# Laying out key and value blocks by DMA, and another order of an attention round

## The chip, the core and the metric

The kernel runs on one core of a Trainium2 chip. The metric is the device time of one execution in microseconds (us). The core has TensorE (PE, matmuls and transposes), VectorE (DVE), ScalarE (ACT), GpSimd (POOL) and SyncE (SP), which here only issues DMA transfers. Each engine runs its own program in order; semaphores tie them together.

## The reference

Two layers over x of 16 batches x 256 tokens x 256 features (4096 tokens), with a context of 16 x 77 x 256:

```
q = layernorm(x) @ Wq + bq;  k, v = split(ctx @ Wkv + bkv)       # 16 heads of 16
out = softmax(q @ k^T / 4) @ v                                    # per batch and head, 77 keys
x = x + out @ Wp + bp
xf = layernorm(layernorm(x)) (with gain and bias)
scores, idx = top_k(xf @ router_w, 2);  gate = softmax(scores)
x = x + sum over the 2 experts of gate * expert(xf)               # 8 experts, hidden 1024
expert(y) = clip((h1 * silu(clip(h2)))) @ Wo + bo,  h1 = ln(y) @ W1 + b1,  h2 = ln(y) @ W2 + b2
```

All in float32. The kernel splits operands of the large matmuls into a high part (float32r) and a low part (the rest) and adds three products.

## The kernel before

The work is cut into 32 tiles of 128 tokens, two for each batch. The first part of the program is a pipeline of **rounds**, numbered -5 to 40. In round i TensorE computes the scores of tile i, the transposed probabilities and the values of tile i-1, the projection of tile i-2, the transposes of `xn` for tile i+3 and of `xf` for tile i-4, and the router's logits of tile i-5. Once for each batch there are also, in an even round, the transposed context, keys and values of batch nb = i//2 + 1, and, in the odd round after it, the queries of that batch. From round 32 on the rounds are interleaved with the first expert tile; then come expert tiles alone. Weights of the first experts are loaded from round 28 on.

Each engine's order in a round is written out by hand: `round_first`, `round_second` and `round_third` for TensorE, a `round_ops` each for ScalarE and VectorE, and loops over the rounds for SP and POOL. The two banks of PSUM called misc are handed round in a fixed order (`misc_turns`): a user of a bank waits until the user before it has been read.

**Scores.** A batch's keys stand in `k_blocks`: on each partition, for each of four heads of a group, the 77 keys if the partition belongs to that head and zeros if not, so that one matmul gives four heads' scores (128 x 308). Scores of half a tile (`m` = 0 or 1) are two such groups in two of three banks, so the second half waits until VectorE has read one bank of the first half (`less_max`). Before, ScalarE writes the high parts of `k_blocks` by copies scaled with a 0/1 mask (line 802), and POOL the low parts by a multiplication with the mask (line 622). The first scores of a batch (line 1537, s = m = 0) wait for both.

**Values.** The 16 x 77 = 1232 keys of a batch stand in 10 blocks of 128 rows; in `v_blocks` each block has 3 places for the heads that it may touch, zero where a row is another head's. A row is 17 floats (16 values and a 1 for the softmax sum). Before, VectorE adds the bias into `v_sb` (77 partitions; line 1189), SP stores it to `v_flat` in HBM (line 456), loads it back in blocks (lines 444 and 447, `v_rep`), and POOL multiplies with masks (line 667). `v_blocks`, `v_sb` and `k_blocks` have two buffers each. `values` (line 1615) of a tile runs in the round after its scores; it ends `round_second`.

**SP's order in a round** before: in an odd round the x load for tile i+7, `load_values`, the store of `x1`; in an even round the x load, the store of `x1`, `store_values` and the context load for batch nb+2.

Of the kernel before, what the change touches and what calls it, by code (L numbers as in the profile page):

```python
# [120 lines left out]
C_KMASK = C_IOTA + P  # L121
C_VMASK = C_KMASK + HPB
C_TOKEN = C_VMASK + KB * BLOCK_HEADS
# [20 lines left out]

def constants():
# [6 lines left out]
    c[:, C_KMASK:C_KMASK + HPB] = (p[:, None] // HD) % HPB == np.arange(HPB)[None, :]  # L152
    for i in range(KB):
        first, n = block_heads(i)
        for j in range(BLOCK_HEADS):
            c[:, C_VMASK + i * BLOCK_HEADS + j] = (i * P + p) // CTX == first + j
# [31 lines left out]
def misc_turns():  # L188

    order = []  # L190
    for i in range(FIRST_ROUND, LAST_ROUND + 1):
        even, nb = i % 2 == 0, i // 2 + 1
        batch = 0 <= nb < BATCH
        uses = [("ctx", nb)] if batch and even else []
        uses += [("attn", i - 2)] if 0 <= i - 2 < NT else []
        uses += [("q", nb)] if batch and not even else []
        uses += [("proj", i - 2)] if 0 <= i - 2 < NT else []
        uses += [("place", i // 2 - 4)] if even and 0 <= i // 2 - 4 < PAIRS else []
        uses += [("xn", i + 3)] if 0 <= i + 3 < NT else []
        uses += [("logits", i - 5)] if 0 <= i - 5 < NT else []  # L200
        uses += [("k", nb), ("v", nb)] if batch and even else []
        uses += [("xf", i - 4)] if 0 <= i - 4 < NT else []
        uses += [("rows", 0), ("rows", 1)] if i == NT - 2 else []
        order += [(i, u) for u in uses]
    turns, last, side = {}, [None, None], 0
    for i, u in order:
        side = 1 if i >= OVERLAP + LAG else 1 - side
        turns[u] = (side, last[side])
        last[side] = u
    return turns, last  # L210


def build(nc, a, out):
    with ExitStack() as ctx:
# [8 lines left out]
        def sems(name, n):  # L223
# [3 lines left out]
        v_flat = nc.dram_tensor("v_flat", [BATCH, KEYS, VW], F32, kind="Internal").ap()  # L227
# [4 lines left out]
        f_vstore, f_vload = sems("f_vstore", 2), sems("f_vload", 2)  # L232
# [4 lines left out]
        (bq_ready, setup_ready, half_ready, zeros_ready, ones_ready, mv_ready) = (  # L237
            sem(n) for n in ("bq_ready", "setup_ready", "half_ready", "zeros_ready",
                             "ones_ready", "mv_ready"))
# [5 lines left out]
        (k_low, k_low_spread, q_low, v_added, v_spread, max_found, less_max, recip_made, attn_made,  # L245
         best_made, best_index) = (
            sem(n) for n in ("k_low", "k_low_spread", "q_low", "v_added", "v_spread", "max_found",
                             "less_max", "recip_made", "attn_made", "best_made", "best_index"))
        (ctx_t_out, k_out, k_high, k_high_spread, xn_t_out, q_out, q_high, exp_made, probs_t_out,
         attn_t_out, xf_t_out, logits_out) = (  # L250
            sem(n) for n in ("ctx_t_out", "k_out", "k_high", "k_high_spread", "xn_t_out", "q_out",
                             "q_high", "exp_made", "probs_t_out", "attn_t_out", "xf_t_out",
                             "logits_out"))
# [70 lines left out]
        k_h = sb("k_h", [P, DC, CTX], F32R)  # L324
        k_l = sb("k_l", [P, DC, CTX])
# [4 lines left out]
        v_rep = [sb(f"v_rep{i}", [P, KB, VW]) for i in range(2)]  # L330
# [92 lines left out]
        def sync_program(e):  # L423
# [15 lines left out]
            def load_values(b):  # L439
                e.wait_ge(f_vstore[b % 2], 16 * (b // 2 + 1))  # L440
                if b >= 2:
                    e.wait_ge(v_spread, 6 * (b - 1))
                full = (KB - 1) * P
                e.dma_start(v_rep[b % 2][:, 0:KB - 1, :],
                            v_flat[b][0:full, :].rearrange("(i p) d -> p i d", p=P)).then_inc(
                                f_vload[b % 2], 16)
                e.dma_start(v_rep[b % 2][0:TAIL, KB - 1, :], v_flat[b][full:KEYS, :]).then_inc(
                    f_vload[b % 2], 16)
# [4 lines left out]

            def store_values(b):
                e.wait_ge(v_added, b + 1)
                e.dma_start(v_flat[b].rearrange("(h k) d -> k h d", h=HEADS),
                            v_sb[b % 2][:, :, :]).then_inc(f_vstore[b % 2], 16)
# [71 lines left out]
            for i in range(FIRST_ROUND, OVERLAP + 2):  # L529
# [67 lines left out]
        def pool_program(e):  # L597
# [19 lines left out]
            def spread_low_keys(b):  # L617
                e.wait_ge(k_low, b + 1)
                if b >= 2:
                    e.wait_ge(scores_mm, SCORES_OF_BATCH * (b - 1))  # L620
                for m in range(DC):
                    e.tensor_tensor(
                        k_blocks[b % 2][:, 1, m, :, :],
                        k_l[:, m, :].unsqueeze(1).broadcast_to([P, HPB, CTX]),
                        const[:, C_KMASK:C_KMASK + HPB].unsqueeze(2).broadcast_to([P, HPB, CTX]),
                        ALU.mult).then_inc(k_low_spread, 1)

# [31 lines left out]
            def spread_values(b):  # L659
                e.wait_ge(f_vload[b % 2], 32 * (b // 2 + 1))  # L660
                if b >= 2:
                    e.wait_ge(values_mm, 2 * b - 2)
                vm = const[:, C_VMASK:C_VMASK + KB * BLOCK_HEADS].rearrange(
                    "p (i j) -> p i j", i=KB)
                for j in range(BLOCK_HEADS):
                    for parts, lo, hi in ((P, 0, KB - 1), (TAIL, KB - 1, KB)):
                        e.tensor_tensor(
                            v_blocks[b % 2][0:parts, lo:hi, j, :], v_rep[b % 2][0:parts, lo:hi, :],
                            vm[0:parts, lo:hi, j:j + 1].broadcast_to([parts, hi - lo, VW]),
                            ALU.mult).then_inc(v_spread, 1)  # L670

# [13 lines left out]

            e.memset(half[:, :], -0.5).then_inc(half_ready, 1)
# [49 lines left out]
            for i in range(FIRST_ROUND, LAST_ROUND + 1):  # L736
                nb = i // 2 + 1
                batch = 0 <= nb < BATCH
                if batch and i % 2:
                    spread_low_keys(nb)  # L740
# [4 lines left out]
                if batch and i % 2:  # L745
                    spread_values(nb)
# [27 lines left out]
        def act_program(e):  # L774
# [8 lines left out]
            def keys(b):  # L783
                ps = misc_of("k", b)
                e.wait_ge(k_mm, b + 1)
                if b:
                    e.wait_ge(k_low, b)
                    e.wait_ge(k_high_spread, HPB * b)
# [6 lines left out]
                e.activation(k_h[:, :, :], k_t[:, :, :], ACTF.Copy).then_inc(k_high, 1)  # L795

            def spread_high_keys(b):
                e.wait_ge(k_high, b + 1)
                if b >= 2:
                    e.wait_ge(scores_mm, SCORES_OF_BATCH * (b - 1))  # L800
                for h in range(HPB):
                    e.activation(k_blocks[b % 2][:, 0, :, h, :], k_h[:, :, :].bitcast(F32),
                                 ACTF.Copy, scale=const[:, C_KMASK + h:C_KMASK + h + 1]).then_inc(
                                     k_high_spread, 1)
# [179 lines left out]
            def round_ops(i):  # L984
# [5 lines left out]
                if batch and even:  # L990
                    ctx_t(nb)
                if 0 <= i - 3 < NT:
                    make_y(i - 3)
                if 0 <= i - 2 < NT:
                    attn_t_copy(i - 2)
                if before:
                    probs_t_copy(i - 1, 1)
                if batch and not even:
                    spread_high_keys(nb)
                    queries(nb)  # L1000
                if before:
                    probs_t_copy(i - 1, 2)
                if 0 <= i + 3 < NT:
                    xn_t_copy(i + 3)
                if 0 <= i - 5 < NT:
                    make_z(i - 5)
                if 0 <= i < NT:
                    exp_scores(i, 1)
                    exp_scores(i, 0)
                if 0 <= i - 5 < NT:  # L1010
                    logits_copy(i - 5)
                if batch and even:
                    keys(nb)
                if 0 <= i - 4 < NT:
                    xf_t_copy(i - 4)
                if 0 <= i + 4 < NT:
                    make_xn(i + 4)
# [58 lines left out]
        def dve_program(e):  # L1076
# [27 lines left out]
            def low_keys(b):  # L1104
                e.wait_ge(k_high, b + 1)
                if b:
                    e.wait_ge(k_low_spread, 2 * b)
                e.tensor_tensor(k_l[:, :, :], k_t[:, :, :], k_h[:, :, :].bitcast(F32),
# [73 lines left out]
            def add_value_bias(b):  # L1182
# [4 lines left out]
                if b >= 2:  # L1187
                    e.wait_ge(f_vstore[b % 2], 16 * (b // 2))
# [170 lines left out]
            def round_ops(i):  # L1359
# [16 lines left out]
                if i == EARLY_TILES + 7:  # L1376
                    early_slots()
                if 0 <= i < NT:
# [23 lines left out]
                if batch and even:  # L1402
                    add_value_bias(nb)
# [113 lines left out]
        def pe_program(e):  # L1517
# [86 lines left out]
            def values(i):  # L1604
# [3 lines left out]
                if i % 2 == 0:  # L1608
                    e.wait_ge(v_spread, 6 * (b + 1))
# [269 lines left out]
```

## Time and profile before

| | |
|---|---|
| median of 3 runs | 1061.42 us (1059.45 to 1069.49) |
| the profiled execution | 1053.62 us, its span 1051.8 us |
| granted clock, mean | 0.947 of full speed |
| TensorE / VectorE / ScalarE / POOL busy | 91% / 75% / 68% / 42% of the span |
| transfers issued by SP for the values of one batch | 3 |

The span is the time from the first to the last instruction. A granted clock of 1.0 is 2.4 GHz for TensorE and 0.5 is 1.2 GHz. In a timeline row the first number is the start (us from the span's start), the second the length of a merged run of instructions, then engine, line, operation, what is written and read, and the count; the bracket is the idle time of that engine just before, and what ended it.

### The profile page before, as it was taken

To read this page: it belongs to the slowest core of one execution; us is meant where nothing else is said; L and a number is where in the kernel's file an instruction comes from. 1 tells how busy PE (TensorE), PEld (TensorE's weight loads), DVE (VectorE), ACT (ScalarE), POOL (GpSimd) and SP (SyncE) were. 2 spreads that over 40 slices of the span, in tenths; PEclk is the share of its full clock that TensorE was granted. 3 is DMA by queue.
4 is the path that set the end of the run, shared out by engine and by line. 5 is a ranking of instruction groups with operands and counts; after the bars stand their busy time and mean duration, and the time that the engine had idled before them with its cause. 6 is when DMAs were issued, how large, how long until landed. Compare 5 with 4: busy or idle time off the path is not lost.

```text
span 1051.8 us, 19535 instructions
## 1 busy us (share of the span) xinstructions
PE 962.4 (91%) x6372; PEld 848.9 (81%) x6372; DVE 790.0 (75%) x1775; ACT 710.2 (68%) x1418; POOL 442.7 (42%) x683
## 2 busy tenths in 40 slices
PE   5999989999987879899999999999999999999893
PEld 4887777777776768688989898888888888889892
DVE  3676777687674677777888787878787878788883
ACT  3777767676665555666777777767676767676781
POOL 4554766777665374512332323223231414050422
PEclk8998989899887789999999999999999999999996
DMA  5312222322226047534656564555555555555644
GB/s 136 50 37 44 61 51 62 76 64 56 52 51 179 21 166 243 147 106 145 168 134 178 127 183 128 165 144 156 153 147 163 139 162 127 175 116 187 169 148 142
DMA packets 124827, 130.42 MB, mean 124 GB/s; under 512 B 50016, under 2 KB 109104, under 8 KB 124592
## 3 DMA queue, kind: packets, MB, share of 16 engines
q1 hardware_dynamic: 111280, 111.13, 35.3%
q0 software_dynamic: 13440, 17.97, 9.6%
q8 instruction: 54, 0.88, 0.3%
q14 instruction: 53, 0.43, 0.1%
HBM read 105.32 MB, written 25.88 MB: 125 GB/s over the span
## 4 chain that ended last, share of the span: by engine, by line
PE 59%; DVE 19%; issue 8%; ACT 5%; DMA 4%; POOL 2%; SPq 1%; another core or an unknown queue 1%; DVEq 0%; ACTq 0%; POOLq 0%
PE bank L1745 25%; PE bank L1775 12%; PE bank L1615 5%; PE bank L1537 3%; DVE wl L1414 3%; DVE maxes L1094 2%; PE bank L1555 2%; PE bank L1582 2%; PE bank L1641 2%; PE bank L1636 2%; DMA raw<-in_W 1%; ACT wh L922 1%; DVE yo L1463 1%; PE bank L1724 1%; DVE xl L1420 1%
## 5 line engine op out<-in xcount | busy, mean ns | idle before, releaser
L730 POOL DMA_INDIRECT out_rows<-yo,token x72 | 125.9, 1748 | 430.3 <-ACT yo L981 415.6
L1745 PE MATMUL bank<-xh,wh 128*128 128x512 f32 (+1 forms) x768 | 267.1, 348 | 17.5 <-DVE hid L1445 14.9
L1745 PE MATMUL bank<-xh,wl 128*128 128x512 f32 (+1 forms) x768 | 262.2, 341 | 0.8 <-issue 0.8
L1745 PE MATMUL bank<-xl,wh 128*128 128x512 f32 (+1 forms) x768 | 261.9, 341 | 0.0
L1414 DVE TENSOR_TENSOR wl<-raw,wh 128x1024 fp32r<-128x1024 f32 x148 | 178.3, 1221 | 37.4 <-ACT wh L922 37.2
L1745 PEld LDWEIGHTS bank<-xh,wh 128*128 128x128 f32 x768 | 147.2, 192 | 37.1 <-DVE hid L1445 19.4
L1775 PE MATMUL bank<-wh,hh 128*128 128x256 f32 x576 | 163.7, 284 | 4.8 <-DVE yo L1463 3.7
L1775 PE MATMUL bank<-wl,hh 128*128 128x256 f32 x576 | 162.5, 282 | 1.5 <-issue 1.5
L1775 PE MATMUL bank<-wh,hl 128*128 128x256 f32 x576 | 162.5, 282 | 0.0
L1745 PEld LDWEIGHTS bank<-xh,wl 128*128 128x128 f32 x768 | 146.7, 191 | 19.0 <-issue 1.2
L922 ACT ACTIVATE wh<-raw 128x1024 fp32r<-128x1024 f32 x148 | 152.8, 1053 | 6.5 <-DMA raw<-in_W 6.5
L1745 PEld LDWEIGHTS bank<-xl,wh 128*128 128x128 f32 x768 | 146.7, 191 | 12.4
L1454 DVE TENSOR_TENSOR hl<-hid,hh 128x512 fp32r<-128x512 f32 x144 | 98.9, 687 | 46.3 <-ACT hh L975 27.0
L1775 PEld LDWEIGHTS bank<-wh,hh 128*128 128x128 f32 x576 | 109.9, 191 | 10.7 <-DVE yo L1463 6.1
L1775 PEld LDWEIGHTS bank<-wl,hh 128*128 128x128 f32 x576 | 110.0, 191 | 4.8 <-issue 1.1
L1775 PEld LDWEIGHTS bank<-wh,hl 128*128 128x128 f32 x576 | 109.9, 191 | 1.2 <-issue 1.2
L975 ACT ACTIVATE hh<-hid 128x512 fp32r<-128x512 f32 x144 | 90.1, 626 | 28.3 <-DVE hid L1449 25.1
L957 ACT ACTIVATE gate_in<-bank,par 128x512 f32<-128x512 f32 x96 | 65.2, 680 | 48.6 <-PE bank L1745 41.8
L981 ACT ACTIVATE yo<-yo,gate 128x256 f32<-128x256 f32 x72 | 31.4, 500 | 92.2 <-DVE yo L1469 92.2
L968 ACT ACTIVATE gate_in<-gate_in 128x512 f32<-128x512 f32 x144 | 89.5, 622 | 0.0
L679 POOL DMA_INDIRECT z_rows<-z,slot x64 | 65.5, 1024 | 42.5 <-issue 26.2
L1615 PEld LDWEIGHTS bank<-v_blocks,probs_t 128*128 128x128 f32 (+1 forms) x640 | 78.8, 202 | 0.2
(161 smaller groups left out, 1922.5 us busy)
## 6 DMA issues: line engine op xcount, KB each, us to landing
raw<-in_W SPq DMA_DIRECT2D x52, 1024.0 KB, 5.0
raw<-in_Wo SPq DMA_DIRECT2D x25, 1024.0 KB
zg<-z_rows SPq DMA_DIRECT2D x12, 520.0 KB, 6.5
xs<-in_x SPq DMA_DIRECT2D x32, 128.0 KB, 3.2
out_rows<-x SPq DMA_DIRECT2D x32, 128.0 KB, 1.7
zg<-z_rows SPq DMA_DIRECT2D x14, 260.0 KB, 3.7
bo_row<-in_bo SPq DMA_DIRECT2D x26, 128.0 KB, 3.5
z_rows<-in_pad SPq DMA_DIRECT2D x8, 260.0 KB
```

The source lines that it names most:

```text
L679: e.indirect_dma_start(out=z_rows, out_offset=bass.IndirectOffsetOnAxis(ap=slot[:, 2 * p + t, k:k + 1], axis=0), in_=z[p % ZR][:, t, :], i ...
L730: e.indirect_dma_start(out=out, out_offset=bass.IndirectOffsetOnAxis(ap=token[j % 4][:, s:s + 1], axis=0), in_=yo[:, s, :], in_offset=None ...
L922: e.activation(wh[j % 2][:, w, c, :], raw[w][:, c, :], ACTF.Copy).then_inc(w_high, 1)
L957: e.activation(dst[:, :], ps[:, 0:WIDTH], ACTF.Identity, bias=par[j % PR][:, X_B2 + u:X_B2 + u + 1]).then_inc(gate_out, 1)
L968: e.activation(gate_in[n % 3][:, :], gate_in[n % 3][:, :], ACTF.Silu).then_inc(silu_made, 1)
L975: e.activation(hh[n % HR][:, :], hid[n % 2][:, :], ACTF.Copy).then_inc(hid_high, 1)
L1414: e.tensor_tensor(wl[j % 2][:, w, c, :], raw[w][:, c, :], wh[j % 2][:, w, c, :].bitcast(F32), ALU.subtract).then_inc(w_low, 1)
L1454: e.tensor_tensor(hl[n % HR][:, :], hid[n % 2][:, :], hh[n % HR][:, :].bitcast(F32), ALU.subtract).then_inc(hid_low, 1)
L1537: mm = e.matmul(score_bank[(u0 + g) % 3][:, 0:HPB * CTX], qs[b % 2][g * HALF:(g + 1) * HALF, m, s * P:(s + 1) * P], k_blocks[b % 2][g * HA ...
L1615: mm = e.matmul(value_bank[:, first * VW:(first + nh) * VW], probs_t[i % 2][0:size, k, :], v_blocks[b % 2][0:size, k, 0:nh, :].rearrange(" ...
L1745: mm = e.matmul(ps[:, h * cols:(h + 1) * cols], ws[j % 2][:, w, c, m * P:(m + 1) * P], xx[j % 2][:, c, 0:cols], start=(h == 0 and c == 0 a ...
L1775: mm = e.matmul(down_bank[s // 2][:, (s % 2) * D:(s % 2 + 1) * D], hs[r][:, at:at + P], ws[q][:, 2, m // 4, (m % 4) * D:(m % 4 + 1) * D], ...
```

## The change

The blocks are zeroed once by POOL, before anything else in its program. From then on transfers write only the parts that aren't zero, from SBUF to SBUF: 8 for the keys of a batch (a head's 16 partitions, high and low part together) and 25 for the values (`VALUE_PARTS`: one for each head, and one more where a head's 77 rows cross a block's border). All 33 are issued by SP in the odd round, values first. `values` of a batch waits for its 25 and the first scores for its 8. The masks, `v_flat`, `v_rep`, and the work of lines 622, 667 and 802 are gone.

In TensorE's round, keys and values move from `round_third` to the end of `round_first`, that is, before the second half of the scores; the context is transposed a round earlier, in `round_third` of the odd round; the logits move before the projection; the transposes of `xn` move behind `values`. ScalarE's and VectorE's orders follow: `exp_scores` of the first half now comes before the queries, and the bias add before VectorE's second softmax half.

```diff
+def value_parts(h):
+    parts, k = [], 0
+    while k < CTX:
+        i, at = divmod(h * CTX + k, P)
+        n = min(CTX - k, P - at)
+        parts.append((k, n, i, at, h - block_heads(i)[0]))
+        k += n
+    return parts
+VALUE_PARTS = [(h,) + part for h in range(HEADS) for part in value_parts(h)]
...
@@ sync_program
-            def load_values(b):
-                e.wait_ge(f_vstore[b % 2], 16 * (b // 2 + 1))
+            def spread_keys(b):
+                e.wait_ge(k_low, b + 1)
+                if b == 0:
+                    e.wait_ge(blocks_ready, 4)
                 if b >= 2:
-                    e.wait_ge(v_spread, 6 * (b - 1))
...
+                    e.wait_ge(scores_mm, SCORES_OF_BATCH * (b - 1))
+                for h in range(HPC):
+                    part = slice(h * HD, (h + 1) * HD)
+                    e.dma_start(k_blocks[b % 2][part, :, :, h % HPB, :].bitcast(F32),
+                                k_parts[part, :, :, :].bitcast(F32)).then_inc(f_kblocks[b % 2], 16)
+            def spread_values(b):
+                e.wait_ge(v_added, b + 1)
+                if b == 0:
+                    e.wait_ge(blocks_ready, 4)
+                if b >= 2:
+                    e.wait_ge(values_mm, 2 * b - 2)
+                for h, k, n, i, at, j in VALUE_PARTS:
+                    e.dma_start(v_blocks[b % 2][at:at + n, i, j, :],
+                                v_sb[b % 2][k:k + n, h, :]).then_inc(f_vblocks[b % 2], 16)
...
                 if batch and i % 2:
-                    load_values(nb)
+                    spread_values(nb)
+                    spread_keys(nb)
+                    if nb + 2 < BATCH:
+                        load_ctx(nb + 2)
                 if 0 <= i - 2 < NT:
                     store_x1(i - 2)
-                if batch and i % 2 == 0:
-                    store_values(nb)
-                    if nb + 2 < BATCH:
-                        load_ctx(nb + 2)
@@ pool_program
+            for i in range(2):
+                e.memset(k_blocks[i][:, :, :, :, :].bitcast(F32), 0.0).then_inc(blocks_ready, 1)
+                e.memset(v_blocks[i][:, :, :, :], 0.0).then_inc(blocks_ready, 1)
...
-                if batch and i % 2:
-                    spread_low_keys(nb)
...
-                if batch and i % 2:
-                    spread_values(nb)
@@ pe_program, scores
-                    e.wait_ge(k_high_spread, HPB * (b + 1))
-                    e.wait_ge(k_low_spread, 2 * (b + 1))
+                    e.wait_ge(f_kblocks[b % 2], 16 * HPC * (b // 2 + 1))
@@ pe_program, the rounds
-                if batch and even:
-                    transpose_ctx(nb)
                 if 0 <= i - 2 < NT:
                     transpose_attn(i - 2)
                 if 0 <= i - 1 < NT:
                     transpose_probs(i - 1, 1)
+                if batch and even:
+                    keys_values(nb)
                 if batch and not even:
                     queries(nb)
...
             def round_second(i):
                 if 0 <= i < NT:
                     scores(i, 1)
                 if 0 <= i - 1 < NT:
                     transpose_probs(i - 1, 2)
+                if 0 <= i - 5 < NT:
+                    route_logits(i - 5)
                 if 0 <= i - 2 < NT:
                     project(i - 2)
...
-                if 0 <= i + 3 < NT:
-                    transpose_xn(i + 3)
                 if 0 <= i - 1 < NT:
                     values(i - 1)
...
             def round_third(i):
-                if 0 <= i - 5 < NT:
-                    route_logits(i - 5)
-                if 0 <= nb < BATCH and even:
-                    keys_values(nb)
+                if i % 2 and 0 <= i // 2 + 2 < BATCH:
+                    transpose_ctx(i // 2 + 2)
+                if 0 <= i + 3 < NT:
+                    transpose_xn(i + 3)
                 if 0 <= i - 4 < NT:
                     transpose_xf(i - 4)
```

## Rows read from the trace of the kernel before

**Rows 1.** The page, busy time of each engine.

```profile
PE 962.4 (91%) x6372; PEld 848.9 (81%) x6372; DVE 790.0 (75%) x1775; ACT 710.2 (68%) x1418; POOL 442.7 (42%) x683
```

**Rows 2.** Windows: length, then busy us of each engine, clock, DMA share, GB/s.

```profile
100.00:200.00 100.00, 90.44 (x668) 76.30 (x664) 74.61 (x265) 71.59 (x195) 69.41 (x126) 0.94 0.29 62
...
200.00:203.00 3.00, 3.00 (x13) 2.66 (x14) 0.84 (x5) 0.75 (x4) 1.99 (x3) 0.50 0.12 44
```

**Rows 3.** Timeline of TensorE, the first scores of batch 0 and of batch 15.

```profile
20.04 0.63 PE L1537 MATMUL bank<-k_blocks,q_h 64*128 64x308 f32 x2 [3.50 <-POOL k_blocks L622]
...
320.05 0.41 PE L1537 MATMUL bank<-k_blocks,q_h 64*128 64x308 f32 x2
```

**Rows 4.** Timeline of TensorE, one period from an even round's scores, clock 1.0.

```profile
213.90 0.41 PE L1537 MATMUL bank<-k_blocks,q_h 64*128 64x308 f32 x2
...
216.81 0.41 PE L1537 MATMUL bank<-k_blocks,q_h 64*128 64x308 f32 x2 [0.84 <-DVE probs L1100]
...
219.63 0.44 PE L1600 MATMUL bank<-const,xn 128*128 128x128 f32 x2 [0.83 <-DVE x L1131]
219.90 2.32 PE L1615 MATMUL bank<-v_blocks,probs_t 128*128 128x34 f32 x20
222.06 0.59 PE L1625 MATMUL bank<-router,xf_t 128*128 128x8 f32 x4
222.50 1.09 PE L1636 MATMUL bank<-c_t,wk 128*128 128x77 f32 x8
...
224.30 0.38 PE L1649 MATMUL bank<-const,xf 128*128 128x128 f32 x2
...
233.32 0.41 PE L1537 MATMUL bank<-k_blocks,q_h 64*128 64x308 f32 x2
```

**Rows 5.** Timeline of TensorE, keys and values to the xf transposes, clock 0.5.

```profile
200.39 1.97 PE L1636 MATMUL bank<-c_t,wk 128*128 128x77 f32 x8
...
203.86 0.63 PE L1649 MATMUL bank<-const,xf 128*128 128x128 f32 x2
```

**Rows 6.** Groups by line, 100 to 300 us; then POOL's timeline in round 29.

```profile
L667 POOL TENSOR_TENSOR v_blocks<-v_rep,const 128x153 f32<-128x153 f32 (+1 forms) x60 | 18.6, 342 | 3.7 <-DMA v_rep<-v_flat 3.4 <-DVE mv L1147 0.2
L802 ACT ACTIVATE k_blocks<-k_h,const 128x154 fp32r<-128x154 f32 x40 | 13.6, 420 | 0.0
...
323.40 2.80 POOL L667 TENSOR_TENSOR v_blocks<-v_rep,const 128x153 f32<-128x153 f32 x6 [5.37 <-DMA v_rep<-v_flat]
```

**Rows 7.** Timeline of SP's issues, in rounds and at the program's start.

```profile
204.55 0.32 SPq L456 DMA_DIRECT2D v_flat<-v_sb  x1
204.92 0.81 SPq L433 DMA_DIRECT2D cs<-in_ctx  x1
...
209.41 0.39 SPq L444 DMA_DIRECT2D v_rep<-v_flat  x1
...
5.46 0.47 SPq L470 DMA_DIRECT2D rows<-in_bv  x1
5.97 0.43 SPq L470 DMA_DIRECT2D rows<-in_bp  x1
```

**Rows 8.** DMA issues (KB, us to landing); then line 522, ns min/median/max.

```profile
out_rows<-x SPq DMA_DIRECT2D x32, 128.0 KB, 1.7
...
v_rep<-v_flat SPq DMA_DIRECT2D x16, 76.5 KB, 2.4
...
v_rep<-v_flat SPq DMA_DIRECT2D x16, 5.3 KB, 2.3
...
L522 SPq DMA_DIRECT2D zg<-z_rows x26: 37/384/390, 319.6 to 1011.5; - x26
```

**Rows 9.** Timelines of VectorE and POOL at the program's start.

```profile
15.62 0.42 DVE L1189 TENSOR_TENSOR v_sb<-bank,rows 77x256 f32<-77x256 f32 x1 [7.72 <-DMA rows<-in_ln_b]
...
0.77 0.31 POOL L687 MEMSET zeros<- 128x256 f32 x1
...
5.33 0.19 POOL L636 TENSOR_TENSOR root<-mv,const 128x3 f32<-128x3 f32 x1 [4.12 <-DVE mv L1157]
```

More of the change, by code:

```diff
@@ L120 @@
 C_IOTA = C_TRI + P
-C_KMASK = C_IOTA + P
-C_VMASK = C_KMASK + HPB
-C_TOKEN = C_VMASK + KB * BLOCK_HEADS
+C_TOKEN = C_IOTA + P
 C_THR_E = C_TOKEN + NT
@@ L151, in constants @@
     c[:, C_IOTA:C_IOTA + P] = p[None, :]
[L152 to L156, printed above, removed]
     c[:, C_TOKEN:C_TOKEN + NT] = p[:, None] + P * np.arange(NT)[None, :]
@@ L193, in misc_turns @@
         batch = 0 <= nb < BATCH
-        uses = [("ctx", nb)] if batch and even else []
-        uses += [("attn", i - 2)] if 0 <= i - 2 < NT else []
+        uses = [("attn", i - 2)] if 0 <= i - 2 < NT else []
+        uses += [("k", nb), ("v", nb)] if batch and even else []
         uses += [("q", nb)] if batch and not even else []
+        uses += [("logits", i - 5)] if 0 <= i - 5 < NT else []
         uses += [("proj", i - 2)] if 0 <= i - 2 < NT else []
         uses += [("place", i // 2 - 4)] if even and 0 <= i // 2 - 4 < PAIRS else []
+        uses += [("ctx", nb + 1)] if 0 <= nb + 1 < BATCH and not even else []
         uses += [("xn", i + 3)] if 0 <= i + 3 < NT else []
-        uses += [("logits", i - 5)] if 0 <= i - 5 < NT else []
-        uses += [("k", nb), ("v", nb)] if batch and even else []
         uses += [("xf", i - 4)] if 0 <= i - 4 < NT else []
@@ L244, in build @@
                              "xf_summed", "xf_var", "z_made", "rstd_step", "rstd_made"))
[L245 to L253, printed above, removed]
+        (k_low, q_low, v_added, max_found, less_max, recip_made, attn_made, best_made,
+         best_index) = (
+            sem(n) for n in ("k_low", "q_low", "v_added", "max_found", "less_max", "recip_made",
+                             "attn_made", "best_made", "best_index"))
+        (ctx_t_out, k_out, k_high, xn_t_out, q_out, q_high, exp_made, probs_t_out, attn_t_out,
+         xf_t_out, logits_out) = (
+            sem(n) for n in ("ctx_t_out", "k_out", "k_high", "xn_t_out", "q_out", "q_high",
+                             "exp_made", "probs_t_out", "attn_t_out", "xf_t_out", "logits_out"))
         (ctx_t_mm, k_mm, v_mm, xn_t_mm, q_mm, scores_mm, probs_t_mm, values_mm, attn_t_mm, proj_mm,
@@ L323, in build @@
         k_t = sb("k_t", [P, DC, CTX])
-        k_h = sb("k_h", [P, DC, CTX], F32R)
-        k_l = sb("k_l", [P, DC, CTX])
+        k_parts = sb("k_parts", [P, 2, DC, CTX], F32R)
         xn = [sb(f"xn{i}", [P, D]) for i in range(2)]
@@ L329, in build @@
         v_sb = [sb(f"v_sb{i}", [CTX, HEADS, VW]) for i in range(2)]
-        v_rep = [sb(f"v_rep{i}", [P, KB, VW]) for i in range(2)]
         k_blocks = [sb(f"k_blocks{i}", [P, 2, DC, HPB, CTX], F32R) for i in range(2)]
@@ L452, in store_x1 @@
                 e.dma_start(out[i * P:(i + 1) * P, :], x1[i % 3][:, :]).then_inc(f_x1[i % 3], 16)
[L454 to L457, printed above, removed]
             e.dma_start(const[:, :], a["const"]).then_inc(f_const, 16)
@@ L615, in make_xf @@
                     xf_made, 1)
[L617 to L626, printed above, removed]
             def roots(r):
@@ L657, in add_bp @@
                     xb_made, 1)
[L659 to L670, printed above, removed]
             def put_rows(p):
@@ L787, in keys @@
                     e.wait_ge(k_low, b)
-                    e.wait_ge(k_high_spread, HPB * b)
+                    e.wait_ge(f_kblocks[(b - 1) % 2], 16 * HPC * ((b + 1) // 2))
                 else:
@@ L794, in keys @@
                 e.wait_ge(k_out, 2 * b + 2)
[L795 to L804, printed above, removed]
+                e.activation(k_parts[:, 0, :, :], k_t[:, :, :], ACTF.Copy).then_inc(k_high, 1)
             def xn_t_copy(i):
@@ L997, in round_ops @@
                     probs_t_copy(i - 1, 1)
+                if 0 <= i - 3 < NT:
+                    make_y(i - 3)
+                if batch and even:
+                    keys(nb)
+                if 0 <= i < NT:
+                    exp_scores(i, 0)
                 if batch and not even:
-                    spread_high_keys(nb)
                     queries(nb)
@@ L1008, in round_ops @@
                     exp_scores(i, 1)
-                    exp_scores(i, 0)
-                if 0 <= i - 5 < NT:
-                    logits_copy(i - 5)
-                if batch and even:
-                    keys(nb)
+                if 0 <= i + 4 < NT:
+                    make_xn(i + 4)
+                if 0 <= nb + 1 < BATCH and not even:
+                    ctx_t(nb + 1)
+                if 0 <= i + 3 < NT:
+                    xn_t_copy(i + 3)
                 if 0 <= i - 4 < NT:
                     xf_t_copy(i - 4)
-                if 0 <= i + 4 < NT:
-                    make_xn(i + 4)
                 p = i // 2 - 4
@@ L1377, in round_ops @@
                     early_slots()
+                if batch and even:
+                    add_value_bias(nb)
                 if 0 <= i < NT:
@@ L1401, in round_ops @@
                     best_experts(i - 6)
-                if batch and even:
-                    add_value_bias(nb)
                 p = (i - 7) // 2
@@ L1608, in values @@
                 if i % 2 == 0:
-                    e.wait_ge(v_spread, 6 * (b + 1))
+                    e.wait_ge(f_vblocks[b % 2], 16 * len(VALUE_PARTS) * (b // 2 + 1))
                 for k in range(KB):
@@ L1674, in round_first @@
                     transpose_probs(i - 1, 0)
-                if batch and even:
-                    transpose_ctx(nb)
                 if 0 <= i - 2 < NT:
@@ L1680, in round_first @@
                     transpose_probs(i - 1, 1)
+                if batch and even:
+                    keys_values(nb)
                 if batch and not even:
@@ L1684, in round_second @@
             def round_second(i):
-                even = i % 2 == 0
                 if 0 <= i < NT:
@@ L1689, in round_second @@
                     transpose_probs(i - 1, 2)
+                if 0 <= i - 5 < NT:
+                    route_logits(i - 5)
                 if 0 <= i - 2 < NT:
                     project(i - 2)
-                if even and 0 <= i // 2 - 4 < PAIRS:
+                if i % 2 == 0 and 0 <= i // 2 - 4 < PAIRS:
                     place_pair(i // 2 - 4)
-                if 0 <= i + 3 < NT:
-                    transpose_xn(i + 3)
                 if 0 <= i - 1 < NT:
@@ L1699, in round_third @@
             def round_third(i):
-                even, nb = i % 2 == 0, i // 2 + 1
-                if 0 <= i - 5 < NT:
-                    route_logits(i - 5)
-                if 0 <= nb < BATCH and even:
-                    keys_values(nb)
+                if i % 2 and 0 <= i // 2 + 2 < BATCH:
+                    transpose_ctx(i // 2 + 2)
+                if 0 <= i + 3 < NT:
+                    transpose_xn(i + 3)
                 if 0 <= i - 4 < NT:
```

26 lines of the change are left out of this document (6 added, 20 removed).

## The prediction

> **What bounds the kernel now.** I read the page first: TensorE is busy 91% of the span [rows 1]. The windows then say where it isn't: in a stretch of attention rounds it is busy 90.4 of 100 us at a granted clock of 0.94 [rows 2]. The change touches only that stretch, from the first scores matmul at 20.04 us to the last one of a new batch at 320.05 us [rows 3]. There are 15 periods of one batch (an even and an odd round) between them, so a period takes (320.05 - 20.04) / 15 = 20.0 us. What follows 320.05 us I leave as it is, but for its shift.
>
> The waits and the TensorE timeline give the inside of a period. In an even round TensorE idles 0.84 us before the second half of the scores, waiting for VectorE's `probs`, and 0.83 us before the `xn` transposes, waiting for `x1` [rows 4]. Keys and values come after `values` and take 224.30 - 222.50 = 1.8 us at the full clock (the xf transposes follow them), and 203.86 - 200.39 = 3.5 us where the granted clock was 0.50, 1.2 of 2.4 GHz [rows 2, 4, 5]. The reader should see two things: the even round has about 1.7 us of holes, and the new order puts 1.8 us of matmuls into the first of them.
>
> **Change, part 1: the order of a round.** Keys and values move ahead of the second half of the scores. That covers the 0.84 us hole; with the xn transposes moved behind `values`, the 0.83 us hole is covered too. If nothing else stood in the way, a full-clock period of 233.32 - 213.90 = 19.4 us [rows 4] would become 19.4 - 1.7 = 17.7 us. The add of the value bias moves before the second softmax half on VectorE: it is a 0.42 us instruction [rows 9], in a hole's length, so I cost it at nothing.
>
> **Part 2: work removed from POOL and ScalarE.** Each batch loses six `v_blocks` multiplies of 0.34 us and two low-key spreads on POOL, and four copies of 0.42 us (1.7 us busy, pipelined) on ScalarE [rows 6]. Neither engine sets the period: TensorE waits for VectorE, and POOL idles in front of these groups. The exception is batch 15, where POOL waited 5.37 us for `v_rep` behind the weight load [rows 6]. That wait goes, but part 3 puts a longer chain in the same place. I count 0 for part 2.
>
> **Part 3: what is added, a long queue on SP.** Before, a batch had three such transfers on SP (one store, two loads). Now it has 25 pieces of values (a piece for each head, and one more where a head crosses a block of 128 rows: 9 crossings) and 8 of keys: 33 transfers, all issued one after the other by SP. The order matters: `spread_values` comes first, and it waits for `values_mm` of the batch two before, which is the last thing TensorE does in the even round. Then the keys, and the next batch's scores wait for all 8 of them to land. Behind them in the queue stand `load_ctx` and the x1 store (needed two and three rounds later; I cost them at nothing) and, in the next round, the x load (seven rounds ahead).
>
> So there is a loop: scores of batch b start; even round up to the end of `values`; 33 issues; landing; scores of batch b+1.
> - Pitch of an issue. A store out of SBUF followed at once by another transfer: 204.55 to 204.92 us, 0.37 us; loads from HBM at the start: 5.46 to 5.97 us, 0.51 us [rows 7]. The new ones read SBUF and are small, so I take 0.37. The lower bound: SP rows of the zg load fall to 37 ns at the least while their median is 384 ns [rows 8], so a much shorter issue can't be excluded; the upper bound is 0.51.
> - Landing after the last issue: 2.3 us for the smallest transfer in the trace (5.3 KB), 1.7 us for an x1 store [rows 8]. I take 2.3.
> - The chain: 32 x 0.37 + 2.3 = 14.1 us.
> - The even round from its scores to the end of `values`: 219.90 + 2.32 - 213.90 = 8.3 us [rows 4]. Take away the two holes (1.7) and the xn transposes (219.90 - 219.63 = 0.3), add keys and values (1.8) and the logits (222.50 - 222.06 = 0.4): some 8.5 us at the full clock. TensorE comes to it after some 4 us of idleness. Before the stretch with the clock of 0.50 TensorE had holes like these; there keys and values alone cost 1.7 us more. I take 1.2 us on top, 9.7 us, and for the range 9.0 to 10.5.
> - Period: 9.7 + 14.1 = 23.8 us. The xf transposes and the odd round (224.30 to 233.32 us, 9.0 us) fit inside the 14.1 us with a microsecond for ctx and xn, which leaves those 4 us of idleness.
>
> **Start.** `v_sb` of batch 0 is ready at 15.62 + 0.42 = 16.0 us, held by the load of the bias rows [rows 9], and this doesn't move. Scores of batch 0 start at 16.0 + 14.1 = 30.1 instead of 20.04 us. Batch 1: scores and cold keys and values (1.1 + 3.5 us), the bias add (0.4), then the chain: 49.2 us. Batches 2 and 3, in rounds that still lack their later work (8.0 and 8.5 us): 71.3 and 93.9 us. Twelve full periods: 93.9 + 12 x 23.8 = 379.5 us, against 320.05: **+59 us**. The four memsets in front of POOL's program are 3,484 elements a partition; the 256 of `zeros` take 0.31 us [rows 9], so at most 4.2 us. POOL's first other work waits for the statistics of x and began at 5.3 us [rows 9]: 0.
>
> **Sum.** 1053.6 us is the profiled execution (span 1051.8 and 1.8 around it), so it becomes about 1113. The median of the three runs is 1061.4, 7.8 above; on that scale the forecast is 1120 us.
>
> **Rivals.**
> A: the chain fits. Between the end of `values` in the even round and the next batch's scores there would be 233.32 - 222.22 - 1.8 + 0.3 = 9.6 us. If 32 pitches and the landing are below that (pitch under 0.23 us), SP hides it all and the reordering pays: 15 x (20.0 - 17.7) = 34 us less, 5 us given back at the start, 1032 us. For it: the single short rows. Against it: the median of [rows 8] and both pairs of [rows 7]. At a pitch near 0.30 both effects cancel (8.5 + 11.6 = 20.1 us a period, and the time is within 1% or so). I give 0.10 to clearly faster and 0.06 to the balance.
>
> B: the DMA engines, not the issue, become the bound. What the trace shows: the load back waits for the store of `v_sb` (77 partitions, 1232 rows of 68 bytes), and starts 209.41 - 204.55 = 4.9 us after it, while the loads back, 1152 rows on 128 partitions, have a median of 2.4 us to landing [rows 7, 8]. Suppose a transfer only divides evenly, so that the number of engines divides its rows. The store is then on 11 engines with 112 rows each, (4.9 - 1.7) / 112 = 0.03 us a row; of the new pieces, with 53 and 23 rows on one engine and others on two or three, the first engine gets 242 rows a batch, 7 us, still below the 9.3 us of their issue. If such a small row costs twice that between two SBUF addresses, the chain is 4 us longer and a period 28 us: 59 + 15 x 4 us, about 1180 us. Chance 0.12.
> The Trainium skill, "DMA: Bandwidth & Descriptors", section "Why a DMA increments its semaphore by 16 and not by 1", says that such a transfer uses the largest number of engines up to 16 that divides its slowest dimension, the lowest-numbered ones, which speaks against pieces cut at odd places; by it the first engine has the most. The trace's 4.9 against 2.4 us agrees with it in direction.
>
> C: the same order, but VectorE becomes the bound (it is busy 74.6 of 100 us [rows 2]), giving about 20 us a period: no change. It needs A's condition, and is inside the 0.06.
>
> **Chances.** Forecast (chain on SP sets the period, 1072 to 1165) 0.72, B 0.12, A 0.10, balance 0.06. One per cent is about what a measurement of this kernel can tell from no change. Faster by over 1%: 0.10; within: 0.07; slower: 0.83. The bounds of the known costs: pitch 0.31 with landing 2.0 and an even round of 9.0 give 20.9 us a period and about +15 us (1076); pitch 0.48 and 10.5 give 28.2 us and about +128 us (1189). The range, 1066 to 1180, leaves out A, the balance's lower part and B's far end.
>
> **What would show it.** SP busy with L-lines of `spread_values` and `spread_keys` for some 12 us a batch without waits between them, at a pitch of 0.37; TensorE's largest wait in front of the first scores of each even round, on the DMA of `k_blocks`, about 4 us, 15 times; scores of batch 0 at about 30 us and of batch 15 at about 380; the 0.84 us wait on `probs` gone from even rounds; the stretch behind batch 15 as long as before. I am wrong if the pitch is well under 0.3 us, if the keys land before the queue has come round, or if the wait for `k_blocks` is far over 4 us, which means the DMA engines and not the issue.

## The result and the profile after

The changed kernel takes 1327.99 us (1325.6 to 1328.79, 4 runs) against 1062.45 us: ratio 1.2484, 95% interval 1.2419 to 1.2548. It is slower, as forecast, but by 266 us and not by 59, and outside the range (1066 to 1180 us). The profiled execution has 1327.55 us and a span of 1325.8.

First the busy times and TensorE's clock in 40 slices, to set beside [rows 1].

```profile
PE 978.4 (74%) x6372; PEld 864.3 (65%) x6372; DVE 787.5 (59%) x1775; ACT 690.9 (52%) x1354; POOL 396.0 (30%) x559
...
PEclk7677766677777766677889999999999999999997
```

TensorE's and VectorE's work is the same to 2%; the span has grown around it, in the first 18 slices (600 us). TensorE's waits in 0 to 620 us (engine, line, what it waited for: us in total, times, longest):

```profile
PE bank L1505 <- issue: 251.7, 15, 18.8
PE bank L1505 <- DMA k_blocks<-k_parts: 21.5, 1, 21.5
PE bank L1505 <- DVE probs L1071: 5.7, 2, 4.7
```

Line 1505 is the scores matmul: 16 waits, one for each batch, 273.2 us in all. The first names the keys' transfers; for the other 15 the profile names nothing ("issue"), and the times below say that they are the same wait. The wait on `probs` is left twice in 620 us, and not in the periods shown. Now TensorE's timeline, answering to [rows 3, 4]: scores of batch 0, one period, a later even round, batch 15.

```profile
42.45 0.62 PE L1505 MATMUL bank<-k_blocks,q_h 64*128 64x308 f32 x2 [21.53 <-DMA k_blocks<-k_parts]
...
146.69 0.63 PE L1505 MATMUL bank<-k_blocks,q_h 64*128 64x308 f32 x2 [16.74 <-issue]
...
154.00 2.31 PE L1583 MATMUL bank<-v_blocks,probs_t 128*128 128x34 f32 x20
...
182.98 0.63 PE L1505 MATMUL bank<-k_blocks,q_h 64*128 64x308 f32 x2 [17.15 <-issue]
...
331.69 0.63 PE L1505 MATMUL bank<-k_blocks,q_h 64*128 64x308 f32 x2 [16.78 <-issue]
...
340.40 2.40 PE L1583 MATMUL bank<-v_blocks,probs_t 128*128 128x34 f32 x20
...
596.10 0.62 PE L1505 MATMUL bank<-k_blocks,q_h 64*128 64x308 f32 x2 [18.79 <-issue]
```

The even round shown first takes 154.00 + 2.31 - 146.69 = 9.6 us (forecast 9.7). It is an early one: the one at 331.69 takes 340.40 + 2.40 - 331.69 = 11.1 us, and from the period at 219.62 us on they take 10.8 to 11.3 us, over the forecast's upper bound of 10.5. From the end of the round at 156.31 to the next batch's scores it is 26.7 us (forecast 14.1). A period is (596.10 - 42.45) / 15 = 36.9 us, and batch 15 starts 276.05 us later than in [rows 3]; the span grew by 274.0. What follows batch 15 took 729.7 us against 731.8. Now SP's timeline for one batch, to set beside [rows 7]:

```profile
156.40 19.84 SPq L461 DMA_DIRECT2D v_blocks<-v_sb  x25
176.36 5.19 SPq L451 DMA_DIRECT2D k_blocks<-k_parts  x8
```

The last of the 8 key issues by itself:

```profile
180.96 0.60 SPq L451 DMA_DIRECT2D k_blocks<-k_parts  x1
```

SP starts 0.09 us after `values` ends at 156.31, and issues without a break until 181.55. 19.96 us for 25 is 0.80 each, 5.19 for 8 is 0.65. The last keys land 1.9 us after 180.96, and the scores start at 182.98: they wait for the keys, and so it is in each of the 16 batches. Both groups over the whole run, ns min/median/max, then landing of the keys:

```profile
L461 SPq DMA_DIRECT2D v_blocks<-v_sb x400: 607/749/968, 16.1 to 588.6; - x134
...
L451 SPq DMA_DIRECT2D k_blocks<-k_parts x128: 585/595/732, 35.8 to 594.1; - x128
...
DMA to landing us min/median/max: 1.9/1.9/2.0
```

Not one of 528 issues is as short as 0.51 us, my upper bound. And the length doesn't follow the rows. Single pieces of batch 3, in the order of the list a piece of 76 rows, of 1, of 77, of 53, of 75 and of 2:

```profile
125.41 0.66 SPq L461 DMA_DIRECT2D v_blocks<-v_sb  x1
126.11 0.61 SPq L461 DMA_DIRECT2D v_blocks<-v_sb  x1
126.76 0.86 SPq L461 DMA_DIRECT2D v_blocks<-v_sb  x1
...
130.81 0.62 SPq L461 DMA_DIRECT2D v_blocks<-v_sb  x1
131.47 0.86 SPq L461 DMA_DIRECT2D v_blocks<-v_sb  x1
132.37 0.65 SPq L461 DMA_DIRECT2D v_blocks<-v_sb  x1
```

53 rows hold SP no longer than 1 row; 75 and 77 rows hold it 0.24 us longer than 53, but 76 rows only 0.04. TensorE's clock fell too: the window 145 to 182 us was granted 0.73 in the mean, against 0.94 over 100 to 200 us before [rows 2].

### The profile page after: what moved, and what is told of

The parts are those of the page before. It is cut to its first block, busy times and chain, and to the rows that moved or that the text cites. A ratio compares the mean times of both kernels' runs of the same rounds, so it can differ in the third digit from the quotient of the medians.

```text
span 1325.8 us, 19771 instructions
## 1 busy us (share of the span) xinstructions
PE 978.4 (74%) x6372; PEld 864.3 (65%) x6372; DVE 787.5 (59%) x1775; ACT 690.9 (52%) x1354; POOL 396.0 (30%) x559
## 4 chain that ended last, share of the span: by engine, by line
PE 53%; issue 25%; DVE 10%; ACT 6%; DMA 3%; SPq 2%; another core or an unknown queue 1%; POOL 0%; ACTq 0%; DVEq 0%; POOLq 0%
PE bank L1711 20%; PE bank L1741 11%; PE bank L1583 4%; PE bank L1523 4%; PE bank L1505 3%; DVE wl L1383 2%; PE bank L1560 2%; PE bank L1604 2%; PE bank L1609 1%; PE bank L1550 1%; SPq L461 1%; ACT wh L894 1%; DMA raw<-in_W 1%; DVE yo L1432 1%
## 5 line engine op out<-in xcount | busy, mean ns | idle before, releaser
L1505 PE MATMUL bank<-k_blocks,q_h 64*128 64x308 f32 x256 | 52.0, 405 | 278.9 <-issue 251.7
L1065 DVE TENSOR_REDUCE maxes<-bank 128x4 f32<-128x308 f32 x128 | 55.4, 473 | 290.5 <-PE bank L1505 283.8
L1505 PEld LDWEIGHTS bank<-k_blocks,q_h 64*128 64x128 f32 x256 | 29.5, 219 | 297.7 <-issue 291.6
L814 ACT ACTIVATE probs_t<-bank 128x512 f32<-128x512 f32 x64 | 38.3, 599 | 291.9 <-PE bank L1523 291.9
L619 POOL TENSOR_TENSOR xf<-y,rows 128x256 f32<-128x256 f32 x32 | 23.6, 737 | 295.8 <-ACT y L858 294.9
## 6 DMA issues: line engine op xcount, KB each, us to landing
k_blocks<-k_parts SPq DMA_DIRECT2D x128, 19.2 KB, 1.9
```

Of the source, the lines that this page charges most:

```text
L814: e.activation(probs_t[i % 2][:, k0:k0 + 4, :], ps[:, :].rearrange("p (j k) -> p j k", k=P), ACTF.Copy).then_inc(probs_t_out, 1)
L1065: e.tensor_reduce(maxes[i % 2][:, hs], view, AXX, ALU.max).then_inc(max_found, 1)
L1505: mm = e.matmul(score_bank[(u0 + g) % 3][:, 0:HPB * CTX], qs[b % 2][g * HALF:(g + 1) * HALF, m, s * P:(s + 1) * P], k_blocks[b % 2][g * HA ...
```

## The experiments

Theory: the 33 issues of SP stand in a row between the end of `values` and the next batch's scores, and each takes 0.6 to 0.9 us by itself, since both of its ends are in SBUF. Rivals: the new order is part of the loss; the DMA engines are behind and hold SP up (case B of the prediction).

**e1_order_only.** The kernel before with the changed `misc_turns`, the changed rounds of TensorE and VectorE, and in ScalarE's:

```
                 if batch and not even:
+                    spread_high_keys(nb)
                     queries(nb)
```

> The new order of a round alone; the blocks are laid out as before, by ScalarE, POOL and the way through HBM. Theory (SP's queue of 33 transfers is the whole loss): with the queue gone a period of a batch is 17.7 to 19 us instead of 20.0, so the time is 15 x 1 to 2.3 us under the kernel before: 1028 to 1047 us. Rival (the new order itself costs, by VectorE's or PSUM's order): 1062 us or more, with a new wait of TensorE inside the even round.

Measured: 1038.07 us, ratio 0.9777 (0.9713 to 0.9841). The new order is no loss but a gain of 23 us, within the theory's range. Scores of batch 0 begin at 22.48 and of batch 15 at 305.78 us, so a period is 18.9 us. An odd and the next even round in TensorE's timeline, and the start of the next period:

```profile
203.68 1.13 PE L1592 MATMUL bank<-wp,attn_t 128*128 128x256 f32 x4 [0.80 <-ACT q_t L823]
...
207.89 0.42 PE L1537 MATMUL bank<-k_blocks,q_h 64*128 64x308 f32 x2
...
209.66 1.01 PE L1636 MATMUL bank<-c_t,wk 128*128 128x77 f32 x8
210.51 1.03 PE L1641 MATMUL bank<-wv,c_t 128*77 128x256 f32 x4
211.47 0.41 PE L1537 MATMUL bank<-k_blocks,q_h 64*128 64x308 f32 x2
...
227.11 0.41 PE L1537 MATMUL bank<-k_blocks,q_h 64*128 64x308 f32 x2
```

Keys and values now fill the place where the second scores had waited 0.84 us [rows 4]: at 211.47 no bracket. A new wait of 0.80 us stands in the odd round, for ScalarE's queries. So at the full clock a period is 227.11 - 207.89 = 19.2 us, only 0.2 less than the 19.4 of [rows 4]. Most of the gain stands elsewhere, as the windows over the 15 periods show, first before the change, then e1 (columns as in [rows 2]):

```profile
20.00:320.00 300.00, 278.74 (x1971) 233.87 (x1971) 215.38 (x738) 208.43 (x561) 194.04 (x365) 0.91 0.27 55
...
22.00:306.00 284.00, 265.53 (x1971) 222.96 (x1973) 221.88 (x741) 205.94 (x564) 196.10 (x364) 0.97 0.28 60
```

TensorE idles 18.5 us instead of 21.3, and the same 1971 matmuls are busy for 265.5 us instead of 278.7, at a mean granted clock of 0.97 instead of 0.91. So some 13 of the 16 us are busy time and go with the clock. All four runs of e1 have a mean clock of 0.961 to 0.969, the seven before it 0.935 to 0.948. Why the new order was granted more clock no run isolates.

**e3_keys_first.**

```
-                    spread_values(nb)
                     spread_keys(nb)
+                    spread_values(nb)
```

> The changed kernel, but SP sends the 8 key transfers ahead of the 25 of the values. Theory (issue time on SP, 33 in a row on the path from values to the next scores): the values have a round to spare, so the period falls from 36.9 us to what SP itself needs for all its issues of a batch, about 27 us, and TensorE's wait moves to the values; scores of batch 0 at about 25 us; 1328 - 15 x 9.9 - 3 = about 1177 us. Rival (DMA engines fall behind, the issue only shows it): the keys land sooner but the period is set by the draining of the pieces, over 30 us, 1230 us or more.

Measured: 1184.9 us (two runs; ratio 1.1165, 1.1073 to 1.1258). A period is 27.7 us (24.24 to 439.14 us), and it is SP's own need:

```profile
208.82 5.19 SPq L451 DMA_DIRECT2D k_blocks<-k_parts  x8
214.11 19.85 SPq L461 DMA_DIRECT2D v_blocks<-v_sb  x25
234.00 0.52 SPq L436 DMA_DIRECT2D cs<-in_ctx  x1
...
236.50 5.17 SPq L451 DMA_DIRECT2D k_blocks<-k_parts  x8
```

236.50 - 208.82 = 27.7 us with no pause over 0.1 us (behind 234.00 stand two stores of `x1` and two loads of x). The swap of two lines gives back 143 of the 266 us: that much was the place of the values ahead of the keys. The rest is the sum of the issues. TensorE's wait moved to the values only in part: over 24 to 440 us it waits 47 us in front of `values` and 45 us in front of the first scores.

**e4_large_pieces.**

```
-VALUE_PARTS = [(h,) + part for h in range(HEADS) for part in value_parts(h)]
+VALUE_PARTS = [(h,) + part for h in range(HEADS) for part in value_parts(h) if part[1] > 28]
```

> The changed kernel without the 9 smaller pieces where a head crosses a block's border (1 to 28 rows each, 159 of 1232 rows; those value rows stay zero). Theory (each issue costs about 0.76 us whatever its rows): 9 x 0.76 = 6.8 us less in each period and at the start, 1328 - 16 x 6.8 = 1219 us. Rival (rows on the DMA engines set it): 13% of the 19.5 us of the values, 2.5 us less each, about 1288 us.

This kernel leaves out work that the result needs: 159 value rows of each batch stay zero.

Measured: 1215.12 us (two runs; ratio 1.145), 113 less; a period is (487.17 - 34.74) / 15 = 30.2 us, 6.7 less. 36% of the pieces with 13% of the rows carried a third of the values' time: the count of the issues weighs, not the rows.

**e5_issue_probe.** The kernel before, with this at the start of SP's program (`landed` waits for all that was sent):

```
+            inside(128, 0)        # SBUF to SBUF: rows, first partition; three each
+            inside(16, 0)
+            inside(77, 0)
+            inside(77, 26)
+            inside(53, 0)
+            inside(1, 0)
+            # then three each: SBUF to HBM 77, back 77, to HBM 128, back 128, to HBM 53
```

> The kernel before, with probes at the very start of SP's program, in threes and with nothing else running, each three followed by a wait for landing: copies of 68-byte rows inside SBUF of 128, 16, 77, 77 (other partitions), 53 and 1 rows; then SBUF to HBM and back with 77 and 128 rows, SBUF to HBM with 53. It shifts everything after it by some 40 us. Theory: the first one of each three inside SBUF already takes 0.6 to 0.9 us, the same for 1 and for 53 rows, so the length is the issue's own; those with HBM on one side take 0.3 to 0.5. Rival (engines behind): the first of three takes 0.3 to 0.4 us and only the later ones more, growing with the rows on one engine.

SP's timeline; the first two lines are transfers of 128 rows, then the first of 16, the first three of 77, the second 77 at other partitions, 53 (first) and 1 row; from 20.16 on HBM is at one end, 77 rows out and back, then 128 out and back:

```profile
0.87 0.59 SPq L467 DMA_DIRECT2D probe_out<-probe_in  x1
1.51 0.59 SPq L467 DMA_DIRECT2D probe_out<-probe_in  x1
...
3.95 0.60 SPq L467 DMA_DIRECT2D probe_out<-probe_in  x1
...
6.98 0.96 SPq L467 DMA_DIRECT2D probe_out<-probe_in  x1
7.99 0.80 SPq L467 DMA_DIRECT2D probe_out<-probe_in  x1
8.84 0.75 SPq L467 DMA_DIRECT2D probe_out<-probe_in  x1
10.71 0.75 SPq L467 DMA_DIRECT2D probe_out<-probe_in  x1
...
14.19 0.64 SPq L467 DMA_DIRECT2D probe_out<-probe_in  x1
...
17.46 0.56 SPq L467 DMA_DIRECT2D probe_out<-probe_in  x1
...
20.95 0.35 SPq L467 DMA_DIRECT2D probe_hbm<-probe_in  x1
22.30 0.28 SPq L467 DMA_DIRECT2D probe_out<-probe_hbm  x1
...
24.50 0.36 SPq L467 DMA_DIRECT2D probe_hbm<-probe_in  x1
26.90 0.32 SPq L467 DMA_DIRECT2D probe_out<-probe_hbm  x1
```

Nothing else ran, and the first of each set, with every earlier transfer landed, is as long as the later ones (0.59, 0.60, 0.75, 0.64, 0.56) or longer (0.96). So nothing was in the way: the length is the issue's own. With HBM at one end the shapes of 53, 77 and 128 rows take 0.24 to 0.43 us. The rival falls. The kernel took 1093.82 us in its one run; its first load was put off by some 32 us, where 40 were expected.

**e2_dma_old_order.** The changed kernel with `misc_turns` and the rounds of all three engines put back. It undoes the order alone.

> The blocks laid out by the 33 transfers as in the changed kernel, but the old order of a round on TensorE, ScalarE and VectorE. Theory (the chain from the end of values through 33 issues to the next scores sets the period): keys and values now stand behind the values of the even round, so the bias add, and with it the first issue, comes 2.5 to 4 us later; even round 9.6 + 3 + 26.6 = 39 us a period instead of 36.9: 1328 + 15 x 2.4 = about 1364 us (1350 to 1380). Rival (the new order makes part of the loss): at or under 1328 us.

Measured: 1342.05 us (two runs; ratio 1.264), 14 us over the changed kernel: the sign is the theory's, but 36 us were expected, and the time is below the expected 1350 to 1380. A period is (612.99 - 42.85) / 15 = 38.0 us. SP waits for the bias add, as expected; below it the even round whose scores start at 189.13 us, `values` on TensorE and the first issue on SP:

```profile
SPq L461 <- DVE v_sb L1158: 48.7, 16, 8.5
...
196.32 2.32 PE L1583 MATMUL bank<-v_blocks,probs_t 128*128 128x34 f32 x20
...
201.36 19.44 SPq L461 DMA_DIRECT2D v_blocks<-v_sb  x25
```

The delay behind `values` is what I had put it at: the first issue comes 201.36 - 198.64 = 2.7 us after their end, against 0.09 in the changed kernel. What I missed is that keys and values then no longer stand ahead of `values`, which so end sooner: 9.5 us after the scores here, 10.4 us in the same period of the changed kernel. In the mean of batches 2 to 15 they end 1.6 us sooner and the issues start 2.6 us later behind them, which leaves 1.0 of the 1.1 us a period.

**e8_values_from_hbm.**

```
-                for h, k, n, i, at, j in VALUE_PARTS: ... v_sb[b % 2][k:k + n, h, :]
+                for h, k, n, i, at, j in VALUE_PARTS: ... v_flat[b][h * CTX + k:h * CTX + k + n, :]
+            def store_values(b): (as before the change; sent in the even round)
```

> The changed kernel, but the values are first stored to HBM in one transfer (in the even round, as before the change) and the same 25 pieces are then loaded from there instead of from SBUF. Theory (a transfer with both ends in SBUF holds SP 0.2 to 0.35 us longer than one with HBM at one end): 25 issues at 0.35 to 0.45 us, 10 us instead of 19.9, a period of 27 us: 1328 - 16 x 9.5 = about 1176 us. Rival (the number of rows and odd pieces makes the length, wherever they come from): 1300 us or more.

Measured: 1190.99 us (two runs; ratio 1.1217), 137 less. The same 25 pieces on the same partitions, a store more, and SP is held half as long:

```profile
211.52 0.38 SPq L459 DMA_DIRECT2D v_flat<-v_sb  x1
...
215.60 9.40 SPq L469 DMA_DIRECT2D v_blocks<-v_flat  x25
225.10 5.06 SPq L454 DMA_DIRECT2D k_blocks<-k_parts  x8
```

9.40 / 25 = 0.38 us a piece, against 0.80. It missed the expectation by 15 us. The first load waits for the store's landing, 28.5 us in 10 waits up to 600 us, for which I had counted nothing; that is more than the miss.

**e10_fitted.** As e8, with `spread_keys` ahead of `spread_values` and VectorE's `low_keys(nb)` moved from the odd round to the end of the even one.

> As e8, and SP sends the keys first, whose low part VectorE makes at the end of the even round instead of in the odd one. Theory: SP needs 5.2 + 25 x 0.42 + about 2.5 = 18.2 us for a batch, and TensorE 19 to 19.5, so the queue is hidden and what is left is the reordering: 1035 to 1055 us. Rival (transfers cost more than their issue, by contention or late landing): over 1080 us.

Measured: 1049.3 us, ratio 0.9864 (0.9826 to 0.9901). The queue fits: in the batch issued at 204 us, 8 and 25 issues take 5.1 and 9.0 us, and SP then waits for the next batch's `k_parts` (10.5 us in 7 waits over 100 to 320 us). A period is (316.37 - 24.45) / 15 = 19.5 us. Laying out by DMA can be hidden, but gives nothing over e1, where POOL and ScalarE do it: it is 11 us slower.

**e6_order_high_early.** e1 with `spread_high_keys(nb)` moved from in front of the queries to the end of ScalarE's even round.

> The new order with the old layout of blocks, as in the first experiment (1038 us), and ScalarE spreads the high keys at the end of the even round, not in front of the queries in the odd one. There TensorE waited 0.8 us in each odd round for ScalarE's queries. Theory (that wait is ScalarE's order): 11 to 15 times 0.8 us less, 1024 to 1032 us. Rival (something else is ready no earlier): 1038 us.

Measured: 1039.41 us, ratio 0.9806 (0.9747 to 0.9866), the same as e1. The wait was ScalarE's order, and is gone; others grew in its place. TensorE's waits of e1 over 20 to 306 us:

```profile
PE bank L1592 <- ACT q_t L823: 8.8, 11, 1.0
...
PE bank L1537 <- DVE probs L1100: 1.1, 2, 1.0
```

and of e6 over 20 to 304 us:

```profile
PE bank L1538 <- DVE probs L1101: 4.2, 6, 1.0
...
PE bank L1538 <- POOL k_blocks L622: 2.3, 1, 2.3
...
21.00:304.00 283.00, 267.15 (x1971) 225.70 (x1973) 219.69 (x740) 207.62 (x564) 194.43 (x362) 0.95 0.29 60
```

I expected 9 to 12 us from this and got none: I took a wait away without asking what was late next. The last line is the window over the 15 periods: beside e1 TensorE idles 15.9 us instead of 18.5, but its busy time is 267.2 us instead of 265.5, at a clock of 0.95 instead of 0.97. So the clock took most of what was left of the gain.

## Why the prediction was wrong

- **The mechanism was right.** The loop that it drew (even round, 33 issues, landing, scores) is the kernel's: 9.6 + 26.7 = 36.3 us in the period shown first, 36.9 us in the mean. SP issues without waits, and the scores wait 16 times. e3 and e4 move the time by what the loop says.
- **The step that failed is the pitch of an issue.** I took 0.37 us and bounded it at 0.51. It is 0.80 for the values and 0.65 for the keys. In place of 32 x 0.37 = 11.8 us there are 24.6 us in the period shown, and 24.3 us in the mean of the 16 batches. 12.4 us more, 16 times, make 199 us of the 217 us by which batch 15's first scores came later than forecast (596.1 against 379.5 us).
- **A second term was too small: the even round.** I took 9.7 us, with 1.2 us for the clock. From 219.62 us on it took 10.8 to 11.3 us, over my 10.5. In the round at 331.69 us, after 16.78 us without work, TensorE's granted clock was 0.53 up to 338.1 us; there keys and values take 3.2 us, against 1.85 us in the round at 146.69. Over all periods this term (scores to first issue) is some 21 us above the forecast. The landing, 2.0 for 2.3 us, gives back 5: 199 + 21 - 5 = 215 us.
- **Why the bound didn't hold.** Every row in [rows 7, 8] has HBM at one end, and even so the load of the context at 204.92 us held SP for 0.81 us, which my bound of 0.51 passed over. In the whole trace before the change the 16 context loads have a median of 0.74 us and the 16 small loads of `v_rep`, whose landing I used, 0.60. None has SBUF at both, and I wrote that a transfer out of SBUF was the nearest, as if reading SBUF made it cheap. e5 has the two side by side, 0.59 against 0.36 us for 128 rows; e8 has it in place, 0.80 against 0.38. An operation with no row in the trace needed a bound well beyond its neighbours. The stated range also stopped at 1180 us, below the 1189 us that my own bounds gave.
- **Rival B gave the right direction of doubt for a wrong cause.** I wrote that a wait far over 4 us would mean the DMA engines; it was 16.7 us and meant the issue. The 0.03 us a row on the first DMA engine plays no part: a piece of 53 rows and one of 1 row take 0.62 and 0.61 us, and e4 follows the count of pieces. But the pieces differ, each with nearly the same length in every batch (median of 16). The Trainium skill's rule on the number of engines ("DMA: Bandwidth & Descriptors", section "Why a DMA increments its semaphore by 16 and not by 1") gives 1 engine to 53 rows, 2 to 2, 11 to 77 and 15 to 75. Sorted by that number the 25 pieces rise, not strictly: 0.61 to 0.62 us at 1 (1, 23 and 53 rows), 0.64 to 0.67 at 2, 0.65 to 0.75 at 3, 0.66 at 4 (76 rows), 0.70 at 5 and 7, 0.73 to 0.76 at 9, 10 and 12, 0.76 to 0.79 at 13 and 14, 0.87 at 15, and 0.77 to 0.89 at 11 (77 rows). But 16 engines (16 or 128 rows) took 0.59 us in e5; the runs show these lengths and not their cause.
- **Right:** the landing, the even round of the early batches, the cover of the 0.84 us hole, nothing for the memsets (POOL's first other work at 5.46 instead of 5.33 us) and for POOL's and ScalarE's lighter load, no change behind batch 15.
- **Part 1 was wrong for the most part.** Its gain of 2.3 us a period was 1.1 us in e1. At the full clock I had 19.4 - 1.7 = 17.7 us and e1 has 19.2: both holes are filled, but new ones take their place (0.80 us for ScalarE's queries is the largest). The other 0.9 us came with the clock, which part 1 did not count.
- **Rival A** failed with the pitch: it needed one under 0.23 us.
- **Where the 266 us are:** 143 come back by sending the keys first (e3), so they are the place of the values in the queue. The rest is the queue's own length, since SP is full at 27.7 us a batch, against 20.0 us a period before and 18.9 us in e1.

The best version is e1, the new order without the DMA layout: 1038.07 us, faster than both kernels. e6 can't be told from it.

## What to carry to other kernels

When many small transfers replace a few large ones, count them, multiply by the issue time of exactly that kind of transfer, and see which queue they stand in and who waits behind them: here 33 issues on a queue that was nearly empty cost more than all the engine work they saved. Put the transfers that are needed first at the head, and undo a combined change part by part, since a good reordering was hidden in this one under a loss more than ten times its size. And look at the granted clock before you put a gain down to a hole that was filled: in e1 most of it was clock.

## What the runs showed of the hardware

- The issue of a transfer from SBUF to SBUF (rows of 68 bytes) held SP 0.59 to 0.60 us with 16 or 128 rows and 0.75 to 0.96 us with 77 in e5, where nothing else ran; with 1 or 53 rows it took 0.55 to 0.65 us in e5 and in the changed kernel. With HBM at one end 53, 77 and 128 such rows took 0.24 to 0.43 us in e5. HBM at one end does not make every issue that short: before the change the context load had a median of 0.74 us.
- In the changed kernel the length did not follow the rows: 76 rows took 0.66 us, 77 rows 0.77 to 0.89, 75 rows 0.87, 74 rows 0.67.
- In e8 25 loads from HBM in a row had a pitch of 9.40 / 25 = 0.38 us; the median of each of the 25 sizes and places was 0.25 to 0.35 us, no longer than e5's loads of 128 rows (0.32 to 0.43 us).
- The same 1971 matmuls of TensorE were busy 278.7 us at a mean granted clock of 0.91 (before) and 265.5 us at 0.97 (e1).
